# A fused adaLN block with routed experts: the sums of gathered parts move behind a low part, one table marks a change of expert, and register loads are done early

## The reference, cut to what matters

```python
scores = jax.nn.sigmoid(xf @ gate_w + bias)
top_scores, top_idx = jax.lax.top_k(scores, K)                 # K = 2 of E = 8
top_scores = top_scores / (jnp.sum(top_scores, axis=-1, keepdims=True) + 1e-06)
w = jnp.zeros((T, E), dtype=xf.dtype).at[jnp.arange(T)[:, None], top_idx].add(top_scores)
up = jnp.einsum('th,ehi->tei', xf, up_w) + up_b
hact = jax.nn.gelu(up, approximate=False)
eo = jnp.einsum('tei,eih->teh', hact, down_w) + down_b
combined = jnp.einsum('teh,te->th', eo * 0.1, w)
shared = (jax.nn.gelu(xf @ sw_up + sb_up, approximate=False) @ sw_down + sb_down) * 0.1
out = (shared + combined).reshape(b, s, h)
out = out / (jnp.max(jnp.abs(out), axis=-1, keepdims=True) + 1e-06)
...
x = x + gb * out
```

## Time and profile before

| | before |
|---|---|
| median of 3 runs | 867.51 us (866.81 to 871.16) |
| the profiled execution, its own time | 869.19 us |
| its span, first to last instruction | 867.4 us |
| mean granted clock of TensorE, share of full | 0.979 |
| share of the span busy: TensorE, VectorE, ScalarE, GpSimd | 96%, 71%, 52%, 53% |
| stage of the experts | from about 433 us to the end |

### The profile page before, as it was taken

One profiled execution on the slowest core, in us unless ns is written; L12 is line 12 of the kernel. 1 busy time (PEld: TensorE's weight loads), 2 busy tenths in 40 slices (PEclk: granted clock), 3 DMA queues, 4 the chain that ended last, 5 costly groups with the idle time before them and its releaser, 6 DMA issues.

```text
span 867.4 us, 21209 instructions
## 1 busy us (share of the span) xinstructions
PE 830.5 (96%) x5973; PEld 777.6 (90%) x5974; DVE 612.7 (71%) x1570; ACT 454.6 (52%) x857; POOL 455.6 (53%) x519
## 2 busy tenths in 40 slices
PE   5999999999999999999989999989999999999993
PEld 5778887889899889888889999989999999999993
DVE  5688988567877687677776667657666667665664
ACT  3765565144444444443666556656555566655550
POOL 4354420124656655765503655554666665665675
PEclk9899999899999999999999999999999999999997
DMA  8220000090422432240671332352344443344543
GB/s 303 75 88 11 0 1 1 12 320 16 125 51 76 125 91 59 100 125 20 227 272 51 102 101 78 90 176 68 86 91 98 94 89 87 77 97 92 101 100 54
DMA packets 68392, 83.08 MB, mean 96 GB/s; under 512 B 22916, under 2 KB 56670, under 8 KB 68192
## 3 DMA queue, kind: packets, MB, share of 16 engines
q0 software_dynamic: 25696, 39.77, 19.7%
q1 hardware_dynamic: 41808, 41.64, 15.3%
q10 hardware_dynamic: 816, 0.79, 0.3%
HBM read 45.43 MB, written 41.29 MB: 100 GB/s over the span
## 4 chain that ended last, share of the span: by engine, by line
PE 59%; issue 6%; DMA 4%; DVE 4%; POOL 3%; ACT 2%; DVEq 1%; ACTq 1%; POOLq 0%; SPq 0%
PE psY L2000 15%; PE psUp L1975 15%; PE psU L1188 10%; PE psY L1200 9%; DMA gx<-shared_part,meta 2%; PE psZ L1128 1%; PE psO L1128 1%; DMA shared_part<-ys,widx 1%; PE psH L1941 1%; ACT gu L2044 1%; PE psZ L1116 1%; POOL out L2320 1%; PE psZ L1107 1%; PE psU L1151 1%; PE psZ L1138 1%
## 5 line engine op out<-in xcount | busy, mean ns | idle before, releaser
L1975 PE MATMUL psUp<-eT,wup 128*128 128x256 f32 x1632 | 204.4, 285 | 7.2 <-DVE eT L2101 4.7
L1975 PEld LDWEIGHTS psUp<-eT,wup 128*128 128x128 f32 x1632 | 200.3, 193 | 8.4 <-issue 8.1
L2000 PE MATMUL psY<-wdn,gTh 128*128 128x256 f32 x1088 | 200.5, 286 | 0.0
L2000 PEld LDWEIGHTS psY<-wdn,gTh 128*128 128x128 f32 x1088 | 169.4, 192 | 0.0
L2000 PE MATMUL psY<-wdn,gTl 128*128 128x256 f32 x544 | 154.3, 284 | 0.0
L2320 POOL DMA_INDIRECT out<-fin,oidx x68 | 109.2, 1606 | 25.4 <-issue 17.5
L2296 POOL DMA_INDIRECT gx<-shared_part,meta x68 | 67.3, 989 | 92.8 <-DMA shared_part<-ys,widx 63.7
L2044 ACT ACTIVATE gu<-psUp,ubias 128x256 f32<-128x256 f32 x272 | 113.4, 468 | 4.4 <-DVE gTl L2106 3.4
L2063 ACT ACTIVATE ys<-yc,meta 128x256 f32<-128x256 f32 x66 | 30.0, 503 | 152.1 <-DVE yc L2129 152.1
L2306 POOL DMA_INDIRECT shared_part<-ys,widx x66 | 68.9, 1044 | 71.8 <-issue 44.6
L2106 DVE TENSOR_TENSOR gTl<-gu,gTh 128x512 fp32r<-128x512 f32 x136 | 93.7, 689 | 18.2 <-ACT gTh L2049 15.6
(11 more groups left out here) (331 smaller groups left out, 1399.4 us busy)
## 6 DMA issues: line engine op xcount, KB each, us to landing
hin<-expert_in SPq DMA_DIRECT2D x36, 256.0 KB
X<-in_L_attn_x SPq DMA_DIRECT2D x8, 512.0 KB, 7.6
X<-bo_row POOLq DMA_DIRECT2D x8, 512.0 KB, 5.6
shared_part<-prow SPq DMA_DIRECT2D x8, 512.0 KB, 5.9
shared_part<-sh SPq DMA_DIRECT2D x8, 512.0 KB
out<-X SPq DMA_DIRECT2D x8, 512.0 KB, 4.7
raw_up<-in_L_ffn_up_w SPq DMA_DIRECT2D x3, 1024.0 KB, 5.2
raw_dn<-in_L_ffn_down_w SPq DMA_DIRECT2D x3, 1024.0 KB, 7.2
```

What stands on the lines that cost most here:

```text
L1975: mm = nc.tensor.matmul(psU[:, c, (m % 2) * TR:(m % 2 + 1) * TR], wup[s][:, a, k, m * P:(m + 1) * P], eT[:, u, b, k], start=(n == 0), stop ...
L2000: mm = nc.tensor.matmul(psE[:, u, h * C:(h + 1) * C], (gTh, gTl)[a][:, u, m, h * P:(h + 1) * P], wdn[s][:, b, m], start=(n == 0), stop=(n ...
```

## The change

- `total(j - 1)` on VectorE moves out of `start`, where it stood right behind `result(j - 1)`, into `end`, behind the low part of chunk 0 of tile j + 1 and ahead of `largest`.
- A new table `utab` (in the memory of `pari`) holds, on the first tile of an expert that has a successor, the successor's number, else 0. ScalarE and VectorE read it in place of `ntab`; its parity is the slot, so that `ahead` there needs no `ktab` and `stab`. `table_slots` gets three more small instructions ahead of the fourth `tab_ok`. SyncE goes on with `ntab` and `ktab`.
- In the opening, ScalarE does chunk 0 of tile 0 first, then `high(1)`, then the two halves of the down weights, one ahead of chunk 1 and one ahead of chunk 2. VectorE does `low(1)` ahead of tile 0's low parts.
- TensorE reads `stab` of tiles 32 to 39 in tiles 0 to 3, two a tile, and `ktab` of tiles 32 to 38 in tiles 30 and 31 (`early`); before, it read both one tile or two ahead from tile 30 on (`soon`). Registers are kept for longer (`known`).

```diff
--- before.py
+++ after.py
@@ -966,6 +966,7 @@
     tcmp = gej[:].rearrange("p j e -> p (j e)")[:, 0:E * NT // 2].rearrange("p (e t) -> p e t", e=E)
     tabf = b2("tabf", [P, 4, ETL], F32)
     pari = b2("pari", [P, ETL], I32)
+    utab = pari
     cap = b2("cap", [P, E], F32)
     dcap = b2("dcap", [P, E], F32)
     prow = b2("prow", [P, ROW], F32)
@@ -1840,7 +1841,7 @@
         if not isinstance(j, int) or j < FULL:
             return entry(eng, table, j, most)
         key = (eng.engine, table.name, j)
-        for old in [k for k in held if k[0] == eng.engine and k[2] < j - 2]:
+        for old in [k for k in held if k[0] == eng.engine and k[2] < j - 2 - ET + FULL]:
             del held[old]
         if key not in held:
             held[key] = entry(eng, table, j, most)
@@ -2003,18 +2004,26 @@
                                     n += 1
                         mm.then_inc(ey_mm, 1)
 
+            def early(j, half):
+
+                if isinstance(j, int) and j < 4:
+                    n = 2 * j + half
+                    if FULL + n <= ET:
+                        known(pe, stab, FULL + n, 2)
+                elif isinstance(j, int) and FULL - 2 <= j < FULL:
+                    for n in (4 * (j - FULL + 2) + 2 * half, 4 * (j - FULL + 2) + 2 * half + 1):
+                        if FULL + n < ET:
+                            known(pe, ktab, FULL + n, E)
+
             turn_h(0, 0, 0)
             up(0, 0, lambda: turn_h(1, 1, 0))
             pe.wait_ge(tab_ok, 4)
 
             def body(j, u, more, i):
-                soon = isinstance(j, int) and FULL - 2 <= j < ET - 2
-                if soon:
-                    known(pe, stab, j + 2, 2)
+                early(j, 0)
                 if more:
                     up(j + 1, 1 - u)
-                if soon:
-                    known(pe, ktab, j + 2, E)
+                early(j, 1)
                 down(j, u, more, i)
 
             tiles(pe, body)
@@ -2024,13 +2033,11 @@
             def ahead(j, new, which):
 
                 with act.If_ne(act.to_reg(new), 0):
-                    k = entry(act, ktab, j, E)
-                    slot = known(act, stab, j, 2)
                     if later(j, 1):
                         wait(act, ey_mm, j)
                     for s in range(2):
-                        with act.If_eq(act.to_reg(slot), 1 - s):
-                            split_hi(act, k + 1, s, which)
+                        with act.If_eq(act.to_reg(new % 2), s):
+                            split_hi(act, new, s, which)
 
             def high(j, u):
                 act.wait_ge(ht_mm, j + 1)
@@ -2064,7 +2071,7 @@
                                          ).then_inc(y_ok, 1)
 
             def body(j, u, more, i):
-                new = entry(act, ntab, j, E - 1)
+                new = entry(act, utab, j, E)
                 if more:
                     e1 = known(act, etab, j + 1, E - 1)
                 if later(j, 1):
@@ -2080,8 +2087,14 @@
                 ahead(j, new, (1,))
 
             high(0, 0)
-            split_hi(act, 0, 0, (1,))
-            chunks(0, 0, entry(act, etab, 0, E - 1), 2)
+            e_first = entry(act, etab, 0, E - 1)
+            chunk(0, 0, e_first, 0)
+            high(1, 1)
+            split_hi(act, 0, 0, (1,), (0,))
+            chunk(0, 0, e_first, 1)
+            split_hi(act, 0, 0, (1,), (1,))
+            chunk(0, 0, e_first, 2)
+            chunk(0, 0, e_first, 3)
             act.wait_ge(tab_ok, 4)
             tiles(act, body)
 
@@ -2090,11 +2103,9 @@
             def ahead(j, new, which):
 
                 with dve.If_ne(dve.to_reg(new), 0):
-                    k = entry(dve, ktab, j, E)
-                    slot = known(dve, stab, j, 2)
                     for s in range(2):
-                        with dve.If_eq(dve.to_reg(slot), 1 - s):
-                            split_lo(dve, k + 1, s, which)
+                        with dve.If_eq(dve.to_reg(new % 2), s):
+                            split_lo(dve, new, s, which)
 
             def low(j, u):
                 dve.wait_ge(ht_hi, j + 1)
@@ -2157,10 +2168,12 @@
                     nc.vector.scalar_tensor_tensor(fin[:, u, h], sm[:, h], top[:, 1, h:h + 1], gate_fb[:],
                                                    ALU.mult, ALU.mult).then_inc(f_s, 1)
 
-            def end(j, u, more):
+            def end(j, u, more, i, e):
 
                 if more:
                     low_g(j + 1, 1 - u, 0)
+                if later(j, 1):
+                    total(j - 1, 1 - u, 16 * i + 16 * u, e)
                 if later(j, 1):
                     largest(j - 1)
                 if more:
@@ -2173,7 +2186,7 @@
             def start(j, u, i):
                 e = known(dve, etab, j - 1, E - 1)
                 result(j - 1, 1 - u, e)
-                total(j - 1, 1 - u, 16 * i + 16 * u, e)
+                return e
 
             def finish(j, u, landed, h, e):
 
@@ -2207,20 +2220,19 @@
                     finish(j - 1, 1 - u, 16 * i + 16 * u, h, e)
 
             def body(j, u, more, i):
-                new = entry(dve, ntab, j, E - 1)
-                if later(j, 1):
-                    start(j, u, i)
+                new = entry(dve, utab, j, E)
+                e = start(j, u, i) if later(j, 1) else 0
                 ahead(j, new, (0,))
                 if more and isinstance(j, int) and j + 1 >= FULL:
                     with needed(dve, j + 1):
-                        end(j, u, True)
+                        end(j, u, True, i, e)
                         low(j + 2, u)
                         low_g(j + 1, 1 - u, MC - 1)
                     with unneeded(dve, j + 1):
-                        end(j, u, False)
+                        end(j, u, False, i, e)
                         low(j + 2, u)
                 else:
-                    end(j, u, more)
+                    end(j, u, more, i, e)
                     if more:
                         low(j + 2, u)
                         low_g(j + 1, 1 - u, MC - 1)
@@ -2236,7 +2248,10 @@
                 link(nc.vector.tensor_scalar(pari[:], ktab[:], 1, None, ALU.bitwise_and))
                 link(nc.vector.tensor_copy(tabf[:, 3], pari[:]))
                 link(nc.vector.scalar_tensor_tensor(tabf[:, 3], gecm[:, :, E - 1], 2.0, tabf[:, 3], ALU.mult, ALU.max))
-                nc.vector.tensor_copy(stab[:], tabf[:, 3]).then_inc(tab_ok, 1)
+                link(nc.vector.tensor_copy(stab[:], tabf[:, 3]))
+                link(nc.vector.tensor_scalar(tabf[:, 0], tabf[:, 0], 1.0, None, ALU.min))
+                link(nc.vector.scalar_tensor_tensor(tabf[:, 1], tabf[:, 1], 1.0, tabf[:, 0], ALU.add, ALU.mult))
+                nc.vector.tensor_copy(utab[:], tabf[:, 1]).then_inc(tab_ok, 1)
 
             def table_used():
                 link(nc.vector.tensor_scalar(used[:], run, 0.0, None, ALU.is_gt))
@@ -2269,9 +2284,9 @@
             low(0, 0)
             table_next()
             table_slots()
+            low(1, 1)
             low_g(0, 0, 0)
             split_lo(dve, 0, 0, (1,), (0,))
-            low(1, 1)
             low_g(0, 0, 1)
             split_lo(dve, 0, 0, (1,), (1,))
             low_g(0, 0, 2)
```

## The result

The changed kernel takes 911.22 us (median of 4 runs, 909.17 to 913.45); the kernel before 867.16 us beside it (4 runs, 865.97 to 871.16). The ratio is 1.0504, with a 95% interval of 1.0473 to 1.0535: slower by about 44 us. The forecast was 915 us, in a range of 897 to 926. The profiled execution of the changed kernel took 912.67 us, with a span of 910.8 us; between the two profiles the span grows by 910.8 - 867.4 = 43.4 us.

The account below looks back on a forecast made before the run. VectorE's turn, closing through ScalarE, was taken to set the pace once lengthened; 44.0 + 3.6 - 2.2 - 1.0 + 4.1 - 2.7 + 1.9 = +47.7 us, giving 915 us, range 897 to 926.

Parts of the forecast that it names:

- What bounds: Expert loop: VectorE's turn is its own loop through ScalarE, mean 11.75 us, only 0.1 to 0.2 us under TensorE's 11.95.
- The move, 2.0 us a plain turn: total() behind chunk 0's low part lengthens VectorE's turn by 2.0 us (1.7 to 2.3); 22 plain turns, +44.0 us.
- Late gathers: Three loop turns whose gathers land late: waiting is given back, so an estimated +1.2 us each, +3.6 us.
- The change of expert: The one turn with a change of expert: loads saved by the single table outweigh total()'s 2.0 us, -2.2 us.
- The opening: Start of the expert stage: earlier gelus and eT, two loads saved, less added table steps; -1.0 us, between 0 and -2.
- First three turns: First three turns of the loop: 2.0 us each, less what late gathers give back; +4.1 us.
- the turn before tile 30: The turn just ahead of tile 30: +1.9 us.
- from tile 30 on: End of the loop: two loads less on TensorE, less idle and full clock, against VectorE's slower turn; -2.7 us.
- TensorE's clock: Expert loop: drops to 1.2 GHz after idling cost 48 matmuls 1.7 us, fitting in 1.9 us idle; nothing added, bound some 10 us.

## Why the prediction was right, step by step

- **What bounds.** VectorE's turn was a loop of its own with 0.1 to 0.2 us in hand against TensorE's, and the busy shares of the earlier trace rows hid it. The runs with one instruction or one load more or less on VectorE settle this: where such a step stands on the path from the low part to the next yc it costs 0.44 to 0.71 us a turn, and in the shadow next to nothing as long as the gather is on time. But VectorE was not the pace of the kernel before by itself. The order of time there, on TensorE and near the end on VectorE:

```profile
737.48 5.92 PE L1975 MATMUL psUp<-eT,wup 128*128 128x256 f32 x48
...
797.21 5.92 PE L1975 MATMUL psUp<-eT,wup 128*128 128x256 f32 x48
...
821.79 0.69 DVE L2129 TENSOR_TENSOR yc<-psY,dbias 128x512 f32<-128x512 f32 x1 [1.71 <-PE psY L2000]
```

  Five turns take TensorE 797.21 - 737.48 = 59.73 us, and between the up matmuls of 581.68 and the gap at 845.53 it lists no idle time; the same five take VectorE 798.44 - 739.97 = 58.47. VectorE, late after the change of expert, closes up on TensorE: its yc comes 739.97 - 737.48 = 2.49 us after TensorE's start of the up matmuls, five turns later 798.44 - 797.21 = 1.23, and from 821.79 on its last four yc wait for the down matmuls. By these lengths an insertion of more than some 0.2 us a turn makes VectorE the pace, while a gain on its path alone is worth little, as the load taken out of the turn without the move shows.
- **The move, 2.0 us a plain turn.** Measured 41.82 / 22 = 1.90. From low part to top it was put at 2.74 us and is 2.68; the lag before top, taken as 0.2, is 752.08 - (751.05 + 0.88) = 0.15. The low part behind eT comes after 0.60 us, as said. In the second turn of a pair it had taken 0.80, so more comes back there than the 0.08 us that the prediction read from the first. Right in the mechanism, and 2 us too high in the sum over 22 turns.
- **Late gathers.** +3.6 predicted, +3.56 measured, in part by luck. The row that was shown gives back 1.26 of 2.0, so +0.74, and that turn grew by 0.73; the sum took 1.2 a turn without a working, and the other two grew by 1.52 and 1.31. Nor had most gathers landed when bs was due, as the prediction read its rows. VectorE's waits in the kernel before from 430 us on:

```profile
DVE bs L2137 <- DMA gx<-shared_part,meta: 18.4, 22, 2.8
```

  22 of the 33 bs of this line waited, 12 of them by less than the 0.74 us that the shadow had to spare. In the changed kernel only the last tile's bs waits for a gather, 1.5 us. The Trainium skill, "DMA: Bandwidth & Descriptors", section "Rules for kernel authors", says to issue a transfer early, compute, and wait on its semaphore late. The trace bears it out as far as these waits go. The price is shown beside it: 2 us of instructions left the time in which VectorE waits for ScalarE in any case.
- **The change of expert.** -2.2 predicted, -2.94 measured. The term was mis-sized: ScalarE's split starts 581.59 - 579.72 = 1.87 us after yc and not 2.3, and VectorE's 2.93 us after and so 3.7 earlier, not 3.2. Alone the table gives 16.54 against 18.90.
- **The opening.** -1.0 predicted, -2.2 measured, and for a reason that was only half there: one split's loads were counted and part of that given away to the new order. Two splits lie on the path and the table shortens both; the new order adds nothing at this start, and its 1.3 us at an earlier one rest on one profile each.
- **First three turns** +4.1 predicted, +3.3 measured; **the turn before tile 30** +1.9 and +1.4; **from tile 30 on** -2.7 and -1.8. At the end TensorE's part was right in kind, but its idle time was put down to two loads where one branch took 2.60 us, and the last gather was left out; it comes late as soon as TensorE is quicker.
- **TensorE's clock.** It was said that a drop after the new idle times would be absorbed. It is: turns with and without one are alike (last section). The idle time itself is 35.0 / 24 = 1.46 us where there is one, and not 1.9.

The sum came to +47.7, the spans differ by 43.4. What was put too high: 2.2 us in the 22 plain turns, 1.2 in the opening, 0.8 in the first three turns, 0.7 at the change of expert, 0.5 in the turn before tile 30; too low by 0.9 from tile 30 on; and 0.2 us lie ahead of the stage. What stays open: how the 6 us of the version without the move divide. The three parts alone give -1.2, -3.9 and -1.6 us by their medians, two of them within what can be told from nothing. That the order's worth depends on when the stage starts is one reason.

## What to carry to other kernels

Before a wait is moved away from where a transfer may be late, see whether the engine waits there for something else anyway: in that shadow the instructions are free as long as they fit, and behind it each of them lengthens the loop. The releaser ahead of the loop's first instruction ("issue" on its own sequencer, or the other engine's matmul), turn by turn, and the lengths of both engines' turns tell which engine paces, better than the busy shares do. And the worth of a saved load or instruction is that of the loop it stands in: the same 0.7 us a turn was worth 21 us where VectorE paced alone and nothing where TensorE stood right behind it.

## What the runs showed that was not expected

**TensorE's clock after short idle times.** In the changed kernel TensorE idles 1.0 to 2.0 us ahead of the up matmuls of most turns, but the granted clock falls to the lower of its two levels, 1.2 GHz, only after some of them: not after 1.70 us at 756, but after 1.82 us at 838 (the two groups of up matmuls above, 6.01 and 7.49 us). Busy time by stretch in the changed kernel (granted clock third from the end):

```profile
756.20:762.00 5.80, 5.80 (x48) 5.80 (x49) 1.70 (x6) 1.45 (x4) 3.26 (x3) 1.00 0.59 136
838.20:845.40 7.20, 7.20 (x48) 7.20 (x49) 2.27 (x7) 2.84 (x7) 4.46 (x4) 0.76 0.66 141
```

With the move alone it falls in every second turn from 621 us on, after idle times of 1.8 to 1.9 us (48 matmuls take 7.48 us at 730.58, 5.92 at 744.02 and 7.49 at 757.93), but not after 2.12 us at 534. A fall costs 48 matmuls some 1.5 us, and the turns in which it falls are no longer, because VectorE paces them; what a fall costs in a kernel in which TensorE is the pace was not run. Which idle time is followed by a fall is not settled by these runs.

**A register load costs more than its own time.** The load takes 0.30 us; out of VectorE's turn it gives 0.71. It is followed on VectorE's sequencer by register instructions of 0.19 and 0.06 us and a check of 0.02, with gaps between them: ahead of the yc at 746.02 in the changed kernel one load starts at 744.3 us and the next at 745.0.

**An earlier start is partly given back.** The expert stage started between 430.6 and 436.6 us in executions of kernels that are the same up to there in all but a few small steps, and between the two profiles of the unchanged kernel about half of the difference came back, with longer waits for transfers: the opening is 1.3 us longer, as is ScalarE's wait for the down weights in it (5.27 and 3.95 us), and the late turns 1.9.
